# Attention of layer 1: two short runs of scores per step, each followed by value products and a sum, in place of one long run

## The chip, the cores and the metric

The kernel runs on one core of a Trainium2 chip. The metric is the device time of one execution in microseconds, here the median of three runs of the kernel before. The span that the profile shows is the time of one execution taken with the profiler on, and it stands a few microseconds beside the median.

## What is computed

Two transformer layers over 4 sequences of 1024 tokens of width 512, with 16 heads of width 32. Layer 0 has attention with a distance bias and an MLP; layer 1 quantises its weights and activations around plain attention. The change touches the attention of layer 1 alone:

```python
attn = jax.nn.softmax(jnp.einsum('bhqd,bhkd->bhqk', q, k) * hd ** (-0.5), axis=-1)
o = jnp.einsum('bhqk,bhkd->bhqd', attn, v).transpose(0, 2, 1, 3).reshape(B, T, D)
```

There are 4 x 16 = 64 heads (batch and head together), each with a 1024 x 1024 score matrix.

## The kernel before

`build_program` runs six stages one after the other, with a barrier of all engines between them. The fifth is `stage_attention1`. Each engine has a program of its own that is written out by hand in step order; engines meet at semaphores only, and each engine works through its own list in order. So the order in `tensor_program` is the order on TensorE.

A head is 8 tiles of 128 queries, and there are 512 tiles in all. A *step* w (the loop variable of every program) takes four tiles, half a head. There are 128 steps of new tiles (NW) and 7 more that empty the pipeline (TAIL).

The scores are computed twice, once for the minimum and once for the exponential:

- `score(u)`, line 720, called **S** below: the 128 x 1024 scores of a query tile, two matmuls of 512 columns, into one of two PSUM buffers `s` of two banks each. `minimum(u)` on VectorE (line 810) reduces them to one number per query and frees the buffer.
- After a head's 8 minima, `minima_halves` on GpSimd (lines 864 and 866) splits them into a high and a low part, `turn_minima` on TensorE (line 756) transposes them, `take_minima` on VectorE (line 816) copies them out, and a DMA puts them as two extra rows beside the queries.
- `score_turned(u, g)`, line 730, called **T**: keys by queries this time, one matmul of 512 columns with the minima already subtracted by the extra rows, into one of three one-bank PSUM buffers `st`. `exponential(u, g)` on ScalarE (line 796) writes exp into `PT` and frees the bank.
- `times_v(u)`, line 741, called **V**: one key block of the value product, four matmuls of the source with 32 output columns each, side by side in the array, 8 matmul instructions in the trace (each of the four is two).
- `add_pair(m)` on GpSimd (line 873) adds two key blocks of `PT`, and `total(m)`, line 749, called a **sum** below, multiplies the result with ones to get the softmax denominators, again 8 matmul instructions. V and sums of one head add up in the two halves of one bank, `po`.
- At the end of a head `take_output` (VectorE, line 823) copies `po`, `turn_output` (TensorE, line 762) transposes it in four matmuls, and `output` (VectorE, lines 833 and 837) divides.

The three `st` banks are a ring that `score_turned`, `turn_minima` and `turn_output` take in the order of their calls. Whoever takes a bank waits until its last user has been read: T waits for the exponential of the taker three places earlier.

Step w before holds, on TensorE: one long run of scores (T S T S TTT S TT S T: 8 T of tiles of step w-4 among 4 S of step w), then `turn_minima` in even steps or `turn_output` in odd ones, then four V of step w-5, and in every even step four sums. An even step is called a minima step below, an odd one an output step; in the steady part every step is one or the other.

Of the kernel before, what the change touches and what calls it, by code (L numbers as in the profile page):

```python
# [12 lines left out]
DC, FC, LT = D // P, F // P, L // P  # L13
# [381 lines left out]
QW = L // 4  # L395
HALF = LT // 2
N_HEADS = B * H
# [245 lines left out]
def stage_attention1(K):  # L643
# [6 lines left out]
    NW, TAIL = N_TILES // 4, 7  # L650
    with Stage(K, "T1") as S:
# [3 lines left out]
        pT = [S.sb(f"PT1{i}", [P, LT, L]) for i in range(2)]  # L655
# [58 lines left out]
        def score(u):  # L714
            n, t = divmod(u, LT)
            p, j = divmod(n, PAIR)
            qs, ks = qs_l.ready(pe, p), ks_l.ready(pe, p)
            ps = ps_r.take(pe, u, (s_min, u + 1))
            for g in range(L // BLK):
                op = nc.tensor.matmul(ps[:, g * BLK:(g + 1) * BLK], qs[0:ROWS, j, t * P:(t + 1) * P],  # L720
                                      ks[0:ROWS, j, g * BLK:(g + 1) * BLK], start=True, stop=True)
            op.then_inc(*s_score.up())

        def score_turned(u, g):
            n, kb = divmod(u, LT)
            p, j = divmod(n, PAIR)
            pe.wait_ge(s_row[n % 2], 32 * (n // 2 + 1))
            pe.wait_ge(s_neg, 1)
            ps = pst_r.take(pe, ("st", u, g), (s_exp, 2 * u + g + 1))
            nc.tensor.matmul(ps[:], ks_l.at[p][0][0:ROWS + 2, j, kb * P:(kb + 1) * P], qs_l.at[p][0][0:ROWS + 2, j, g * BLK:(g + 1) * BLK],  # L730
                             start=True, stop=True).then_inc(*s_st.up())

        def times_v(u):
            n, kb = divmod(u, LT)
            p, j = divmod(n, PAIR)
            v = v_l.ready(pe, p)
            pe.wait_ge(s_exp, 2 * u + 2)
            if kb == 0:
                pe.wait_ge(s_ov, n)
            for g in range(4):  # L740
                op = nc.tensor.matmul(po[g * HD:(g + 1) * HD, 0:QW], v[:, kb, j * HD:(j + 1) * HD],  # L741
                                      pT[n % 2][:, kb, g * QW:(g + 1) * QW], start=kb == 0, stop=kb == LT - 1)
            op.then_inc(*s_pv.up())

        def total(m):
            n, k = divmod(m, LT // 2)
            pe.wait_ge(s_two, m + 1)
            for g in range(4):
                op = nc.tensor.matmul(po[g * HD:(g + 1) * HD, QW:2 * QW], K.ones[:, 0:HD], two[m % 6][:, g * QW:(g + 1) * QW],
                                      start=k == 0, stop=k == LT // 2 - 1)  # L750
            op.then_inc(*s_sum.up())

        def turn_minima(n):
            ps = pst_r.take(pe, ("min", n), (s_mr, n + 1))
            pe.wait_ge(s_mm, n + 1)
            nc.tensor.transpose(ps[0:2 * LT, 0:P], mm[n % 2][:].bitcast(F32).rearrange("p a t -> p (a t)"), K.ident[:]).then_inc(*s_mt.up())

        def turn_output(n):
            ps = pst_r.take(pe, ("out", n), (s_out, n + 1))
            pe.wait_ge(s_ov, n + 1)  # L760
            for i in range(2 * QW // P):
                op = nc.tensor.transpose(ps[:, i * P:(i + 1) * P], ov[n % 2][:, i * P:(i + 1) * P], K.ident[:])
            op.then_inc(*s_turn.up())

        def tensor_program():
            n_turned = n_first = 0
            for w in range(NW + TAIL):
                for turned, first in ((1, 1), (1, 1), (3, 1), (2, 1), (1, 0)):
                    if 0 <= w - 4 < NW:
                        for _ in range(turned):  # L770
                            score_turned(*divmod(8 * (w - 4) + n_turned, 2))
                            n_turned = (n_turned + 1) % 8
                    if w < NW and first:
                        score(4 * w + n_first)
                        n_first = (n_first + 1) % 4
                n, odd = divmod(w - 2, 2)
                if not odd and 0 <= n < N_HEADS:
                    turn_minima(n)
                n, odd = divmod(w - 7, 2)
                if not odd and 0 <= n < N_HEADS:  # L780
                    turn_output(n)
                if 0 <= w - 5 < NW:
                    for i in range(4):
                        times_v(4 * (w - 5) + i)
                n, odd = divmod(w - 6, 2)
                if not odd and 0 <= n < N_HEADS:
                    for i in range(LT // 2):
                        total(n * LT // 2 + i)

        def exponential(u, g):  # L790
            n, kb = divmod(u, LT)
# [13 lines left out]
        def minimum(u):  # L805
            n, t = divmod(u, LT)
            if t == 0 and n >= 2:
                dve.wait_ge(s_mm, n - 1)
            dve.wait_ge(s_score, u + 1)
            nc.vector.tensor_reduce(mn[n % 2][:, t:t + 1], ps_r.at[u][:], AX.X, ALU.min).then_inc(*s_min.up())  # L810

        def take_minima(n):
            if n >= 2:
                dve.wait_ge(s_row[n % 2], 32 * (n // 2))
            dve.wait_ge(s_mt, n + 1)
            nc.vector.tensor_copy(mr[n % 2][:], pst_r.at["min", n][0:2 * LT, 0:P]).then_inc(*s_mr.up())

        def take_output(n):
            dve.wait_ge(s_pv, (n + 1) * LT)
            dve.wait_ge(s_sum, (n + 1) * LT // 2)  # L820
            if n >= 2:
                dve.wait_ge(s_turn, n - 1)
            nc.vector.tensor_copy(ov[n % 2][:], po[:]).then_inc(*s_ov.up())

        def output(n):
            h = n % H
            buf = og.room(dve, n // GRP)
            ps = pst_r.at["out", n]
            dve.wait_ge(s_turn, n + 1)
            if n >= 2:  # L830
                dve.wait_ge(s_out, n - 1)
            sums = ps[:, 2 * P:4 * P].rearrange("p (i g d) -> p i g d", i=2, d=HD)[:, :, :, 0]
            nc.vector.reciprocal(rec[n % 2][:], sums).then_inc(*s_rec.up())
            dve.wait_ge(s_rec, n + 1)
            hc = slice(h % GRP * HD, (h % GRP + 1) * HD)
            for i in range(2):
                op = nc.vector.tensor_tensor(buf[:].rearrange("p (g i) d -> p i g d", i=2)[:, i, :, hc],
                                             ps[:, i * P:(i + 1) * P].rearrange("p (g d) -> p g d", d=HD),
                                             rec[n % 2][:, i, :].unsqueeze(2).to_broadcast([P, 4, HD]), ALU.mult)
            op.then_inc(*s_out.up())  # L840

        def vector_program():
            for w in range(NW + TAIL):
                if w < NW:
                    minimum(4 * w)
                    minimum(4 * w + 1)
                n, odd = divmod(w - 7, 2)
                if not odd and 0 <= n < N_HEADS:
                    take_output(n)
                if w < NW:  # L850
                    minimum(4 * w + 2)
                    minimum(4 * w + 3)
                n, odd = divmod(w - 2, 2)
                if not odd and 0 <= n < N_HEADS:
                    take_minima(n)
                n, odd = divmod(w - 7, 2)
                if not odd and 0 <= n < N_HEADS:
                    output(n)

        def minima_halves(n):  # L860
            pool.wait_ge(s_min, (n + 1) * LT)
# [25 lines left out]

        sync_program()
        tensor_program()
        vector_program()  # L890
        scalar_program()
        gpsimd_program()
# [1297 lines left out]
```

## Time and profile before

| | us |
|---|---|
| median of 3 runs | 3895.55 (3895.14 to 3897.41) |
| profiled execution, span | 3899.1 |
| stage of the change, in the span | 2553 to 3523, 970 |
| TensorE busy, whole span | 3604.4 (92%) |
| VectorE / ScalarE / GpSimd busy, whole span | 2538.2 / 2259.6 / 1668.4 |

The profile gives, per engine, busy time and what an idle engine was waiting for. PE is TensorE's matmul, PEld its weight load (which may run beside a matmul), DVE VectorE, ACT ScalarE, POOL GpSimd. PE's matmuls overlap, so that a busy PE isn't a PE at its full rate. What a wait costs is better read from the starts of successive matmuls and from PEld's idle time.

### The profile page before, as it was taken

What the parts mean: (1) busy time and instruction counts of PE and PEld (TensorE: products, weight loads), DVE (VectorE), ACT (ScalarE), POOL (GpSimd) and SP (SyncE); (2) the same over time, 40 slices, a digit from 0 to 9 for tenths busy, and PEclk for the clock granted to TensorE, in tenths of its full rate; (3) what the DMA queues carried; (4) which work ended last, traced back from release to release, by engine and by line L of the source; (5) the groups of instructions that cost most, each with busy time, mean ns of one, the idle gap of its engine ahead of it and who ended that gap; (6) DMA issues with size and microseconds to landing.
All of it is one profiled execution on the core that took longest, in us unless ns stands there. A gap on an engine that the chain in (4) does not pass through costs nothing. (4 is left out here: it accounts for less than half of the span.)

```text
span 3899.1 us, 67913 instructions
## 1 busy us (share of the span) xinstructions
PE 3604.4 (92%) x25868; PEld 2519.1 (65%) x25924; DVE 2538.2 (65%) x4159; ACT 2259.6 (58%) x3899; POOL 1668.4 (43%) x1931
## 2 busy tenths in 40 slices
PE   8997999999999988699999995979999999995999
PEld 6885767677777766578778873546666666652555
DVE  4335888888888867334431116857777777765987
ACT  2225888888888856222222225835555555554988
POOL 0004555555555547000000006746666666663554
PEclk9998999999999999899999997979999999997999
DMA  5546333333333159444431116853333333414221
GB/s 188 185 162 157 64 69 64 69 64 69 64 69 63 31 174 320 134 149 159 157 130 54 54 42 212 314 122 78 74 69 74 78 69 71 81 31 136 77 82 50
DMA packets 309604, 419.91 MB, mean 108 GB/s; under 512 B 90472, under 2 KB 167788, under 8 KB 309274
## 3 DMA queue, kind: packets, MB, share of 16 engines
q1 hardware_dynamic: 309280, 415.56, 38.3%
q8 instruction: 207, 3.39, 0.4%
q14 instruction: 117, 0.96, 0.1%
HBM read 257.34 MB, written 157.32 MB: 106 GB/s over the span
## 5 line engine op out<-in xcount | busy, mean ns | idle before, releaser
L796 ACT ACTIVATE PT<-st 128x512 f32<-128x512 f32 x1024 | 545.2, 605 | 420.9 <-PE st L730 417.5
L634 POOL TENSOR_SCALAR biastile<-dist,ascale 128x1024 f32<-128x1024 f32 x512 | 577.1, 1127 | 487.3 <-DVE mn L588 474.5
L810 DVE TENSOR_REDUCE mn<-s 128x1 f32<-128x1024 f32 x512 | 596.6, 1216 | 274.1 <-PE s L720 274.0
L873 POOL TENSOR_TENSOR two<-PT 128x1024 f32<-128x1024 f32 x256 | 603.4, 2376 | 306.8 <-ACT PT L796 306.6
L588 DVE CUSTOM_DVE_ANT_0 Sn<-sp,biastile 128x1024 f32<-128x1024 f32 x512 | 622.1, 1215 | 78.4 <-PE pt L521 46.6
L559 ACT ACTIVATE Sn<-Sn,mn 128x1024 f32<-128x1024 f32 x512 | 586.8, 1146 | 19.0 <-DVE mn L588 19.0
L521 PEld LDWEIGHTS pt<-ident,Sn 128*128 128x128 f32 x4096 | 455.2, 141 | 177.5 <-issue 151.0
L521 PE MATMUL pt<-ident,Sn 128*128 128x128 f32 x4096 | 546.9, 277 | 22.0 <-DVE og L601 22.0
L549 ACT ACTIVATE PT<-pt 128x512 f32<-128x512 f32 x576 | 338.0, 599 | 135.6 <-PE pt L521 125.8
L1335 ACT ACTIVATE gf<-pf,b1T 128x512 f32<-128x512 f32 x128 | 88.3, 690 | 542.2 <-PE pf L1280 529.6
L730 PE MATMUL st<-QS,KS 98*128 98x512 f32 x1024 | 377.4, 426 | 1.2 <-ACT PT L796 1.2
L720 PE MATMUL s<-KS,QS 96*128 96x512 f32 x1024 | 353.5, 428 | 25.6 <-DMA KS<-s_khi 23.8
L551 DVE COPY PT<-pt 128x512 f32<-128x512 f32 x448 | 309.8, 692 | 88.2 <-PE pt L521 81.5
L1426 DVE TENSOR_TENSOR gl<-gf,gh 128x512 fp32r<-128x512 f32 x128 | 88.6, 692 | 381.3 <-ACT gh L1339 378.9
L1741 POOL MEMSET rcD<- 128x128 bf16 x2 | 0.3, 206 | 781.2 <-POOLq L131 781.2
L489 PE MATMUL sp<-KS,QS 97*128 97x512 f32 x1024 | 304.8, 418 | 23.6 <-DMA KS<-cpad 18.8
L510 PE MATMUL po<-PT,Vp 128*32 128x256 f32 x4096 | 273.7, 384 | 27.6 <-ACT ov L572 27.6
L730 PEld LDWEIGHTS st<-QS,KS 98*128 98x128 f32 x1024 | 192.6, 188 | 146.2 <-ACT PT L796 65.1
L741 PE MATMUL po<-PT,Vp 128*32 128x256 f32 x4096 | 248.8, 384 | 0.0
L720 PEld LDWEIGHTS s<-KS,QS 96*128 96x128 f32 x1024 | 177.2, 194 | 99.4 <-DVE mn L810 51.7
L1291 PE MATMUL pacc<-w2h,gh 128*128 128x512 f32 x512 | 203.5, 397 | 4.2 <-DVE gl L1426 4.2
L489 PEld LDWEIGHTS sp<-KS,QS 97*128 97x128 f32 x1024 | 174.2, 191 | 50.2 <-issue 19.2
(257 smaller groups left out, 6169.1 us busy)
## 6 DMA issues: line engine op xcount, KB each, us to landing
QS<-s_qhi SPq DMA_DIRECT2D x128, 256.0 KB, 4.9
KS<-s_khi SPq DMA_DIRECT2D x128, 256.0 KB, 6.8
KS<-s_klo SPq DMA_DIRECT2D x64, 256.0 KB, 6.1
QS<-s_qlo SPq DMA_DIRECT2D x64, 256.0 KB, 6.8
Vp<-s_v SPq DMA_DIRECT2D x64, 256.0 KB, 7.5
s_o<-og SPq DMA_DIRECT2D x32, 512.0 KB, 4.0
xA<-in_x SPq DMA_DIRECT2D x8, 1024.0 KB, 5.8
s_qhi<-qstage SPq DMA_DIRECT2D x32, 256.0 KB, 2.0
```

Of the source, the lines that this page charges most:

```text
L489: op = nc.tensor.matmul(ps[:, g * BLK:(g + 1) * BLK], qs[0:rows_s, j, t * P:(t + 1) * P], ks[0:rows_s, j, g * BLK:(g + 1) * BLK], start=Tr ...
L521: op = nc.tensor.transpose(ps[:, i, :], sn[:, (g * HALF + i) * P:(g * HALF + i + 1) * P], K.ident[:])
L549: nc.scalar.activation(dst, src, ACT.Copy).then_inc(*s_cp_act.up())
L551: nc.vector.tensor_copy(dst, src).then_inc(*s_cp_dve.up())
L559: nc.scalar.activation(sn[:], sn[:], ACT.Exp, scale=-1.0, bias=mn[n % 3][:, t:t + 1], accum_out=sums[n % 5][:, t:t + 1]).then_inc(*s_exp.up())
L588: nc.vector.tensor_tensor_reduce(sn[:], sp_r.at[s][:], bt[s % 2][:], 1.0, 3.4e38, ALU.add, ALU.min, m).then_inc(*s_min.up())
L634: nc.gpsimd.tensor_scalar(bt[s % 2][:], dist[:, t, :], K.ascale[:, n % H:n % H + 1], 1.0, ALU.mult, ALU.mult).then_inc(*s_bias.up())
L720: op = nc.tensor.matmul(ps[:, g * BLK:(g + 1) * BLK], qs[0:ROWS, j, t * P:(t + 1) * P], ks[0:ROWS, j, g * BLK:(g + 1) * BLK], start=True, ...
L730: nc.tensor.matmul(ps[:], ks_l.at[p][0][0:ROWS + 2, j, kb * P:(kb + 1) * P], qs_l.at[p][0][0:ROWS + 2, j, g * BLK:(g + 1) * BLK], start=Tr ...
L796: nc.scalar.activation(pT[n % 2][:, kb, g * BLK:(g + 1) * BLK], pst_r.at["st", u, g][:], ACT.Exp, scale=-1.0).then_inc(*s_exp.up())
L810: nc.vector.tensor_reduce(mn[n % 2][:, t:t + 1], ps_r.at[u][:], AX.X, ALU.min).then_inc(*s_min.up())
L873: nc.gpsimd.tensor_tensor(two[m % 6][:], pT[n % 2][:, 2 * k, :], pT[n % 2][:, 2 * k + 1, :], ALU.add).then_inc(*s_two.up())
```

## The change

The long run becomes two runs. Each has two S and four T in the order S T S T T T, then (in the first run alone) the transposes of minima or of output, then two V and one sum. Sums move from four in every second step to one in each run, one step after the step in which their head's V were all done before; they now share the bank `po` with V that are still adding, so the first sum of a head no longer starts an accumulation of its own. VectorE's order follows: `take_output` goes ahead of the step's first minimum, `output` and `take_minima` between the second and the third.

```diff
         def tensor_program():
-            n_turned = n_first = 0
             for w in range(NW + TAIL):
-                for turned, first in ((1, 1), (1, 1), (3, 1), (2, 1), (1, 0)):
-                    if 0 <= w - 4 < NW:
-                        for _ in range(turned):
-                            score_turned(*divmod(8 * (w - 4) + n_turned, 2))
-                            n_turned = (n_turned + 1) % 8
-                    if w < NW and first:
-                        score(4 * w + n_first)
-                        n_first = (n_first + 1) % 4
-                n, odd = divmod(w - 2, 2)
-                if not odd and 0 <= n < N_HEADS:
-                    turn_minima(n)
-                n, odd = divmod(w - 7, 2)
-                if not odd and 0 <= n < N_HEADS:
-                    turn_output(n)
-                if 0 <= w - 5 < NW:
-                    for i in range(4):
-                        times_v(4 * (w - 5) + i)
-                n, odd = divmod(w - 6, 2)
-                if not odd and 0 <= n < N_HEADS:
-                    for i in range(LT // 2):
-                        total(n * LT // 2 + i)
+                for run in range(2):
+                    for k in range(4):
+                        if k < 2 and w < NW:
+                            score(4 * w + 2 * run + k)
+                        if 0 <= w - 4 < NW:
+                            score_turned(*divmod(8 * (w - 4) + 4 * run + k, 2))
+                    if run == 0:
+                        n, odd = divmod(w - 2, 2)
+                        if not odd and 0 <= n < N_HEADS:
+                            turn_minima(n)
+                        n, odd = divmod(w - 7, 2)
+                        if not odd and 0 <= n < N_HEADS:
+                            turn_output(n)
+                    if 0 <= w - 5 < NW:
+                        times_v(4 * (w - 5) + 2 * run)
+                        times_v(4 * (w - 5) + 2 * run + 1)
+                        total(2 * (w - 5) + run)
...
         def vector_program():
             for w in range(NW + TAIL):
+                n, odd = divmod(w - 7, 2)
+                out = not odd and 0 <= n < N_HEADS
+                if out:
+                    take_output(n)
                 if w < NW:
                     minimum(4 * w)
                     minimum(4 * w + 1)
-                n, odd = divmod(w - 7, 2)
-                if not odd and 0 <= n < N_HEADS:
-                    take_output(n)
+                if out:
+                    output(n)
+                m, odd = divmod(w - 2, 2)
+                if not odd and 0 <= m < N_HEADS:
+                    take_minima(m)
                 if w < NW:
                     minimum(4 * w + 2)
                     minimum(4 * w + 3)
```

In `total` the matmuls' `start=k == 0` becomes `start=False`; in it and in `times_v` a flag for the build's own bookkeeping is set, which is no instruction.

## Rows read from the trace of the kernel before

**Rows 1.** Busy time by stretch: the stage, and ten pairs of steps (all engines)

```profile
core 0: us, PE busy (x) PEld busy (x) DVE busy (x) ACT busy (x) POOL busy (x), PEclk, DMA share, GB/s
2553.00:3523.00 970.00, 960.00 (x8512) 582.93 (x8512) 680.40 (x830) 545.19 (x1024) 628.14 (x385) 0.98 0.34 70
...
3100.00:3247.00 147.00, 147.00 (x1338) 90.27 (x1330) 106.21 (x130) 85.30 (x160) 97.90 (x60) 1.00 0.35 72
```

**Rows 2.** Waits in two pairs of steps, 2999.53 to 3028.93: total us, times, longest

```profile
PEld st L730 <- ACT PT L796: 1.9, 8, 0.3
PEld st L730 <- issue: 1.6, 4, 0.4
PEld s L720 <- DVE mn L810: 1.3, 6, 0.3
```

**Rows 3.** Timeline of PE, an output step: start, us until its last end, xcount

```profile
3011.95 0.50 PE L730 MATMUL st<-QS,KS 98*128 98x512 f32 x1
3012.29 0.63 PE L720 MATMUL s<-KS,QS 96*128 96x512 f32 x2
3012.76 0.39 PE L730 MATMUL st<-QS,KS 98*128 98x512 f32 x1
...
3013.45 0.89 PE L730 MATMUL st<-QS,KS 98*128 98x512 f32 x3
...
3016.18 0.60 PE L762 MATMUL st<-ident,ov 128*128 128x128 f32 x4
3016.71 0.42 PE L741 MATMUL po<-PT,Vp 128*32 128x256 f32 x4
```

**Rows 4.** Timeline of PE, the end of the minima step before it

```profile
3008.16 0.27 PE L756 MATMUL st<-ident,mm 128*16 128x128 f32 x1
3008.36 1.93 PE L741 MATMUL po<-PT,Vp 128*32 128x256 f32 x32
3010.11 1.91 PE L749 MATMUL po<-two,ones 128*32 128x256 f32 x32
```

**Rows 5.** Timeline of weight loads in the output step, with idle time before each

```profile
3011.95 0.19 PEld L730 LDWEIGHTS st<-QS,KS 98*128 98x128 f32 x1 [0.41 <-issue]
...
3015.08 0.19 PEld L730 LDWEIGHTS st<-QS,KS 98*128 98x128 f32 x1 [0.30 <-ACT PT L796]
...
3016.06 0.48 PEld L762 LDWEIGHTS st<-ident,ov 128*128 128x128 f32 x4 [0.16 <-ACT PT L796]
```

**Rows 6.** Timeline of ScalarE in the output step

```profile
3012.57 1.22 ACT L796 ACTIVATE PT<-st 128x512 f32<-128x512 f32 x2 [3.62 <-PE st L730]
3013.95 3.04 ACT L796 ACTIVATE PT<-st 128x512 f32<-128x512 f32 x6 [0.15 <-PE st L730]
```

**Rows 7.** Timeline of VectorE in the output step

```profile
3012.96 2.36 DVE L810 TENSOR_REDUCE mn<-s 128x1 f32<-128x1024 f32 x2 [3.21 <-PE s L720]
3015.23 0.68 DVE L823 COPY ov<-po 128x512 f32<-128x512 f32 x1
```

**Rows 8.** Timeline of GpSimd, 3000 to 3018

```profile
3000.41 4.70 POOL L873 TENSOR_TENSOR two<-PT 128x1024 f32<-128x1024 f32 x2 [3.37 <-ACT PT L796]
...
3005.36 0.20 POOL L866 TENSOR_TENSOR mm<-mn,mm 128x8 fp32r<-128x8 f32 x1
...
3015.11 4.72 POOL L873 TENSOR_TENSOR two<-PT 128x1024 f32<-128x1024 f32 x2 [3.37 <-ACT PT L796]
```

**Rows 9.** Timeline of PE, step 5, where V follows T directly

```profile
2589.63 0.39 PE L730 MATMUL st<-QS,KS 98*128 98x512 f32 x1
2589.95 1.93 PE L741 MATMUL po<-PT,Vp 128*32 128x256 f32 x32
```

**Rows 10.** Timeline of PE, step 128: eight T without S between them

```profile
3489.12 0.96 PE L730 MATMUL st<-QS,KS 98*128 98x512 f32 x3
3490.39 2.51 PE L730 MATMUL st<-QS,KS 98*128 98x512 f32 x5 [0.31 <-ACT PT L796]
```

**Rows 11.** The V of step 128 as a stretch: us, PE busy, PEclk, DMA share, GB/s

```profile
3493.15:3496.33 3.18, 3.18 (x33) 0.54 0.14 38
```

More of the change, by code:

```diff
@@ L741, in times_v @@
                 op = nc.tensor.matmul(po[g * HD:(g + 1) * HD, 0:QW], v[:, kb, j * HD:(j + 1) * HD],
-                                      pT[n % 2][:, kb, g * QW:(g + 1) * QW], start=kb == 0, stop=kb == LT - 1)
+                                      pT[n % 2][:, kb, g * QW:(g + 1) * QW], start=kb == 0, stop=kb == LT - 1,
+                                      skip_group_check=True)
             op.then_inc(*s_pv.up())
@@ L749, in total @@
                 op = nc.tensor.matmul(po[g * HD:(g + 1) * HD, QW:2 * QW], K.ones[:, 0:HD], two[m % 6][:, g * QW:(g + 1) * QW],
-                                      start=k == 0, stop=k == LT // 2 - 1)
+                                      start=False, stop=k == LT // 2 - 1, skip_group_check=True)
             op.then_inc(*s_sum.up())
@@ L852, in vector_program @@
                     minimum(4 * w + 3)
[L853 to L858, printed above, removed]
         def minima_halves(n):
```

## The prediction, made before the changed kernel ran

> **What bounds the kernel now.** I read the stretches of busy time first. The stage of the change takes 970 us of the span, and TensorE is busy for 960 of them; VectorE, the next, for 680 [rows 1]. Ten pairs of steps take 147.0 us, so a pair (a minima step and an output step) takes 14.70 us, at a granted clock of 1.00; per pair VectorE works 10.6 us, GpSimd 9.8 and ScalarE 8.5 [rows 1]. No other engine can set the pace by its load. But a busy matmul row says nothing of the rate, so the waits come second. In two pairs the score runs' weight loads waited 1.9 us for exponentials, 1.3 us for minima, and 1.6 us for "issue", that is, for nothing that the profile names [rows 2]. The last stands 4 times, once per step, and one of them is the way back from V and sums to the scores [rows 5]: the engine changes from 32 output columns to 128 there, and from 128 to 32 on the way in. Such a change is called a border below.
>
> So the change buys a shorter queue of scores (fewer waits for ScalarE and VectorE) and pays with more borders. Third, the timelines give the price of each. All times below count from the start of the first score matmul of a run.
>
> **What the rows give.** *Spacing in a run:* T, S, S start at 3012.76 and the next T at 3013.45, 0.23 each [rows 3]. *V and sums:* 32 instructions of V take 1.75 us from start to start of what follows, 32 of the sums 1.84 up to the next score [rows 3, 4]. A fourth of it is 0.44 for one V and 0.43 for one sum; the sums' 1.84 has about 0.11 of border in it. *The border in:* T directly before V takes 0.32 [rows 9] where T before a score takes 0.23, so 0.09. *The border out:* these 0.11, and then 0.34 from the first score matmul to the second (3011.95 to 3012.29 [rows 3]) in place of 0.23, 0.11 more. With 0.02 for V's slower first group a round trip costs 0.33 us.
>
> The first weight load after the border starts at 3011.95, together with its matmul and after 0.41 us idle [rows 5]; nothing was loaded ahead. The Trainium skill, page "TensorE: Matmul & The Clock Gate", section "Step-by-step: what each phase is for", has TensorE pull a weight load ahead of matmuls in flight when it goes to the background weight buffer. By that rule the border would be all but free and the added time 40 us less than in my sum (60 pairs x 2 borders x 0.33). The trace disagrees here, and another page, "TensorEngine Tiling (Array Packing)", section "Key Properties", says that changing the tiling mode drains the engine, which is what the row shows.
>
> *ScalarE's answer:* a T's exponential starts 0.43 us after the T (3012.76 to the second of the pair at 3013.19), 0.49 where a wait for another semaphore stands ahead (3013.45 to 3013.95), takes 0.60, and exponentials in a row start 0.49 apart [rows 3, 6]. The bank's next weight load starts 0.05 later: the fourth exponential ends at 3015.04, the load is at 3015.08 [rows 5, 6]. For the transpose the matmul comes 0.12 after its load [rows 3, 5]. *VectorE's answer:* a minimum starts 0.43 after the second matmul of its S and takes 1.2 [rows 3, 7]. *GpSimd:* a pair addition starts 0.07 after the fourth exponential's end and takes 2.36 to 2.39; the split of the minima ends 0.45 after the addition ahead of it (3005.11 to 3005.56) [rows 6, 8].
>
> **A check on these prices:** the minima step before, by the same steps. T0 0; S 0.34, 0.57; T1 0.81; S 1.04, 1.27; T2 to T4 1.50, 1.74, 1.98. The third S waits for the first minimum, 0.57 + 0.43 + 1.22 + 0.05 = 2.29, against 2.21 without. T5 2.86, T6 3.13; the fourth S waits for the second minimum, 3.47; T7 3.99; transpose 4.22; V 4.43; sums 6.18; end 8.02. The output step is 4.22 + 0.53 (four transposes to V, 3016.18 to 3016.71 [rows 3]) + 1.86 = 6.61. Together 14.63 against 14.70 measured.
>
> **The change, part by part, for a pair.**
> Removed and added instructions: none of weight. Every S, T, V, sum and transpose is there before and after, and VectorE, ScalarE and GpSimd do the same work. `rows_to_queries` and the loads on SP wait for the same events, of which the minima come earlier; each head's T are two steps away, so nothing hangs on it. A head's first sum without its own start flag is no other instruction.
> *Without any wait* a run is S T S T T T: S 0, 0.34; T0 0.57; S 0.81, 1.04; T1 1.27; T2 1.51; T3 1.74. A second run then has V at 2.06, and two V, a sum and the border take 0.88 + 0.43 + 0.11 = 1.43 (with the first group): 3.49. The first run of an output step: transposes at 1.97, V at 2.50, end 3.93. Of a minima step: transpose 1.97, V 0.20 later [rows 4] at 2.17, end 3.60. The pair: 3.60 + 3.93 + 2 x 3.49 = 14.51. So even with no wait left, the gain is 0.19 per pair: the two new round trips (0.66) eat most of the 0.85 that waits cost now (14.70 less 14.51 - 0.66).
> *Added wait 1, T3 in each run.* It takes T0's bank. T0 0.57 + 0.49 + 0.60 + 0.05 = 1.71 for its load, the matmul about 0.08 later: 1.79 in place of 1.74. I take 0.05 x 4 runs = 0.20 (bounds 0 and 0.3).
> *Added wait 2, the transposes.* Before, two T and two S stood between them and the T whose bank they take. Now T2 and T3 alone do. T1 1.27 + 0.43 = 1.70, + 0.60 = 2.30, + 0.05 load, + 0.12 matmul = 2.47, against 1.79 + 0.23 = 2.02: **0.45 per step, 0.9 per pair**. Eight T with nothing between them show this wait already: the fourth comes 1.27 after the first and waited 0.31 [rows 10]. What is queued behind it on TensorE is all of the rest, V and the next run. Bounds: 0.35 (if the small load of the minima is faster) and 0.5 each.
> *Added wait 3, the minima's split.* The transpose of the minima moves from the end of the step to its first half, and GpSimd's list has the split behind the pair additions of the step before. In the second run of a step the exponentials start 1.06, 1.70, 2.18, 2.67, so the last ends at 3.27; GpSimd adds from 3.34 to 5.73, which is 2.19 into the next step (a second run is 3.49 + 0.05 = 3.54); the split ends at 2.64, and the transpose starts at about 2.80 in place of 2.47. That is 0.33 per pair. Bounds 0 (if the addition starts earlier) and 0.5.
> *VectorE:* `take_output` copies `po` from 0.2 to 0.9 of an output step (0.68 [rows 7]), ahead of the transposes; the first minimum moves by 0.1, and the third S comes over 4 us after the first. `output` ends near 4.2, and the T that wants its bank comes at 5.9. Cost nothing; if the cover went, some 0.1 us.
> Sum per pair: 14.51 + 0.20 + 0.90 + 0.33 = 15.94, or 1.24 more than 14.70. Steps 8 to 127 are 60 pairs: +74 to +75 us, and I take 75. Filling and emptying: steps 5 to 7 lose about 2 us (added borders), the last five win about 2 (T in fours, not eights, wait less for ScalarE [rows 10]), both estimates. Nothing net.
> 3899.1 + 75 = 3974 for the profiled execution; the median lies 3.5 lower, so 3895.6 + 75 = **3971**.
>
> **Rivals.**
> *B, the split of the minima isn't late* (GpSimd starts its additions earlier than I think), or T3 doesn't wait: 15.4 to 15.65 per pair, +42 to +57 us, 3938 to 3953. For it: GpSimd has 6 us per pair free. Against: it can't start before the fourth exponential.
> *C, not slower: the waits vanish.* Short runs are what three banks can hold, and with 14.51 per pair the kernel would be 11 us faster, 3884. It decides at the transposes: they must find T1's bank free within 0.75 us of T1, where the rows give 1.08. Waits of under 0.19 per pair in all are the point of break-even. Little speaks for it.
> *D, the border is hidden by the load ahead:* 40 us less than the forecast, 3931.
> *E, the clock falls.* In all of the 147 us above it is 1.00 (2.4 GHz) [rows 1]. Where eight T in a row were paced by ScalarE at the end [rows 10], it fell to the 1.2 GHz level, and the V after that took 3.18 us at 0.54 [rows 11] in place of 1.75 [rows 4]. If one step in eight ran so, each would lose about 4 us, +64 on top, 4035. The same page of the Trainium skill, section "A second HAM failure mode: psum-queue depth-cycling", tells of such a clock going up and down from small idle times between groups of matmuls. By it this change, which adds idle time, would get E. Against: the pair now has 0.85 us of waits and 0.66 us of borders with no fall; with the change it has 1.43 and 1.32 us in 15.9.
> *F, further waits that I don't see* (VectorE's new order, semaphores on TensorE): another 0.3 or more per pair, 3990 to 4010.
>
> **Chances:** forecast (3957 to 3988) 0.64, B 0.16, C 0.04, D 0.03, E 0.03, F 0.07, no difference 0.03. The range of 3936 to 3992 takes in B and the bounds of the waits, and leaves out some 0.17. A measurement of this kernel tells about 0.2% (8 us) from no change: faster 0.04, within it 0.03, slower 0.93.
>
> **What the changed profile would show.** A pair of steps of 15.9 to 16.0 us. The idle time of "issue" at the borders 4 times per step in place of 2. Weight loads of the transposes (lines for minima and output) waiting 0.4 to 0.8 us each, the longest for ScalarE and GpSimd; hardly any wait of S for minima. A second run of 3.5 us. I would be wrong if the transposes didn't wait (then 3880 to 3910), if T3 waited much longer than 0.05, or if the granted clock in the steady part were below 1.00.

## The result and the profile after

| | before | changed |
|---|---|---|
| median | 3896.48 (4 runs) | 3971.67 (3969.42 to 3974.57, 4 runs) |
| ratio | | 1.0194, interval 1.0179 to 1.0208 |
| profiled execution, span | 3899.1 | 3967.6 |
| stage, first score to last output transpose | 2559.0 to 3522.5, 963.5 | 2551.8 to 3590.7, 1038.9 |
| a pair of steps, steady part | 14.71 | 15.93 |

The changed kernel is 75.2 us slower, and the stage is 75.4 us longer. The profiled spans differ by 68.5 alone: in the changed kernel's profile the stage begins 7.2 us earlier, after code that the change doesn't touch. In the ten kept profiles, all with the same code ahead of the stage, it begins anywhere from 2547.5 to 2559.0. A span's difference holds such scatter of other stages; the pair of steps, 60 times repeated, doesn't, and is what the experiments below are read from.

The stretches of the changed kernel answer to [rows 1]; columns are length, busy time of PE, PEld, DVE, ACT and POOL, granted clock, DMA share, GB/s. TensorE is now without work for 0.6 us of a pair. Each of the other engines is busy for much the same time per ten pairs as before (VectorE 108.2 us against 106.2, ScalarE 87.0 against 85.3, GpSimd 99.0 against 97.9):

```profile
3100.00:3259.30 159.30, 153.22 (x1331) 89.25 (x1331) 108.17 (x130) 86.97 (x160) 98.96 (x61) 1.00 0.33 69
2999.92:3015.84 15.92, 15.32 (x137) 8.93 (x133) 10.80 (x13) 8.69 (x16) 9.92 (x7) 1.00 0.03 5
```

The waits of two pairs, 2999.92 to 3031.77, answer to [rows 2]:

```profile
PEld st L730 <- ACT PT L792: 2.2, 8, 0.3
PEld s L720 <- issue: 2.1, 5, 0.4
PEld st L757 <- ACT PT L792: 1.5, 2, 0.8
...
PEld po L741 <- issue: 1.3, 6, 0.2
PEld s L720 <- DVE mn L806: 1.2, 3, 0.4
PE st L757 <- POOL mm L862: 1.0, 2, 0.5
PEld st L763 <- ACT PT L792: 0.9, 2, 0.4
```

The two transposes (L757 minima, L763 output) now wait, the minima's for GpSimd in the end. The row "DVE mn" is not what it says. Call the border from V and sums back to scores or transposes the way out, and the one into V the way in: two rows of the weight loads' timeline show the same 0.41 us at the way out, once put to "issue" and once to a minimum that had ended at 3007.41, half a microsecond before. The 5 and the 3 together are the 8 ways out of four steps, where before there were 4. So no score waits for a minimum any more.

```profile
3004.28 0.30 PEld L720 LDWEIGHTS s<-KS,QS 96*128 96x128 f32 x2 [0.41 <-issue]
...
3007.87 0.30 PEld L720 LDWEIGHTS s<-KS,QS 96*128 96x128 f32 x2 [0.41 <-DVE mn L806]
```

The timeline of PE over the pair (start, us until its last end, xcount) answers to [rows 3] and [rows 4]. The four runs start at 2999.92, 3004.28, 3007.87 and 3012.24, and the next pair at 3015.84:

```profile
2999.92 0.73 PE L720 MATMUL s<-KS,QS 96*128 96x512 f32 x2
3000.49 0.39 PE L730 MATMUL st<-QS,KS 98*128 98x512 f32 x1
3000.73 0.62 PE L720 MATMUL s<-KS,QS 96*128 96x512 f32 x2
3001.19 0.97 PE L730 MATMUL st<-QS,KS 98*128 98x512 f32 x3
3002.65 0.27 PE L757 MATMUL st<-ident,mm 128*16 128x128 f32 x1 [0.49 <-POOL mm L862]
3002.85 1.07 PE L741 MATMUL po<-PT,Vp 128*32 128x256 f32 x16
...
3004.28 0.73 PE L720 MATMUL s<-KS,QS 96*128 96x512 f32 x2
...
3005.56 0.95 PE L730 MATMUL st<-QS,KS 98*128 98x512 f32 x3
3006.44 1.07 PE L741 MATMUL po<-PT,Vp 128*32 128x256 f32 x16
...
3007.87 0.73 PE L720 MATMUL s<-KS,QS 96*128 96x512 f32 x2
...
3010.22 0.66 PE L763 MATMUL st<-ident,ov 128*128 128x128 f32 x4
3010.81 1.07 PE L741 MATMUL po<-PT,Vp 128*32 128x256 f32 x16
...
3012.24 0.73 PE L720 MATMUL s<-KS,QS 96*128 96x512 f32 x2
```

GpSimd's timeline shows why the minima's transpose is late [rows 8]. The addition of the step before ends at 3002.05, 2.13 us into the step; the split ends at 3002.50, and the transpose runs at 3002.65:

```profile
2999.67 2.38 POOL L869 TENSOR_TENSOR two<-PT 128x1024 f32<-128x1024 f32 x1 [1.98 <-ACT PT L792]
3002.02 0.20 POOL L860 TENSOR_SCALAR mm<-mn 128x8 fp32r<-128x8 f32 x1
3002.30 0.20 POOL L862 TENSOR_TENSOR mm<-mn,mm 128x8 fp32r<-128x8 f32 x1
```

### The profile page after: what moved, and what is told of

Same layout as the page of the kernel before. It is cut to its first block and busy times, and to the rows that moved or that the text cites. A ratio compares the mean times of both kernels' runs of the same rounds, so it can differ in the third digit from the quotient of the medians.

```text
span 3967.6 us, 67969 instructions
## 1 busy us (share of the span) xinstructions
PE 3640.0 (92%) x25924; PEld 2507.2 (63%) x25924; DVE 2552.0 (64%) x4159; ACT 2270.3 (57%) x3899; POOL 1674.9 (42%) x1931
## 5 line engine op out<-in xcount | busy, mean ns | idle before, releaser
L792 ACT ACTIVATE PT<-st 128x512 f32<-128x512 f32 x1024 | 556.0, 598 | 487.3 <-PE st L730 483.1
L730 PE MATMUL st<-QS,KS 98*128 98x512 f32 x1024 | 350.6, 423 | 2.4 <-ACT PT L792 2.4
L510 PE MATMUL po<-PT,Vp 128*32 128x256 f32 x4096 | 273.7, 384 | 27.6 <-ACT ov L572 27.6
L741 PE MATMUL po<-PT,Vp 128*32 128x256 f32 x4096 | 274.9, 386 | 0.0
```

The costliest lines, as they stand in the source:

```text
L792: nc.scalar.activation(pT[n % 2][:, kb, g * BLK:(g + 1) * BLK], pst_r.at["st", u, g][:], ACT.Exp, scale=-1.0).then_inc(*s_exp.up())
```

## Experiments

The theory M is the prediction's sum: two new borders per pair, and three new waits that more than take the place of those removed. Its main rival is that the borders alone carry the loss (and its opposite, D, that they cost nothing). "Pair" is the mean over 50 pairs in the steady part; medians of the first four stand against a kernel before of 3893.38 us on their chip, those of the last four against 3894.97.

| kernel | pair, expected | pair, measured | median | over before |
|---|---|---|---|---|
| x4_border | 15.25 to 15.35 | 15.22 | 3924.79 | 1.0078 (1.0063 to 1.0093) |
| x1_turns_later | 14.9 | 14.79 | 3897.22 | 1.0009 (1.0000 to 1.0018) |
| x5_minima_later | 15.57 | 15.57 | 3944.95 | 1.0131 (1.0116 to 1.0146) |
| x2_t_first | 15.2 | 15.21 | 3925.18 | 1.0080 (1.0063 to 1.0097) |
| x8_both | 14.40 | 14.41 | 3877.86 | 0.9953 (0.9941 to 0.9966) |
| x3_tfirst_min_later | 14.51 | 14.55 | 3883.47 | 0.9970 (0.9961 to 0.9980) |
| x7_sums_in_fours | 16.36 | 16.37 | 3997.96 | 1.0264 (1.0250 to 1.0278) |
| after_again | 15.93 | 15.92 | 3966.82 | 1.0188 (1.0172 to 1.0203) |

### The border by itself

On the kernel before:

```diff
-                n, odd = divmod(w - 2, 2)
-                if not odd and 0 <= n < N_HEADS:
-                    turn_minima(n)
-                n, odd = divmod(w - 7, 2)
-                if not odd and 0 <= n < N_HEADS:
-                    turn_output(n)
-                if 0 <= w - 5 < NW:
-                    for i in range(4):
-                        times_v(4 * (w - 5) + i)
+                for run in range(2):
+                    if run:
+                        n, odd = divmod(w - 2, 2)
+                        if not odd and 0 <= n < N_HEADS:
+                            turn_minima(n)
+                        n, odd = divmod(w - 7, 2)
+                        if not odd and 0 <= n < N_HEADS:
+                            turn_output(n)
+                    if 0 <= w - 5 < NW:
+                        for i in range(2):
+                            times_v(4 * (w - 5) + 2 * run + i)
```

> The kernel before, its one long run of scores and its sums kept; only the transposes of minima and output move from the end of the scores to between the second and the third V, so that every step has one more change from 32 output columns to 128 and back, and nothing else new. My sum (a round trip costs 0.27 to 0.33 us per step, 128 steps): a pair of steps of 15.25 to 15.35 us, +35 to +42 us on before, 3932 to 3938. If weight loads hide the border (rival D): within 8 us of before. If the borders carried the whole +75 of the change (two more in it than in before per pair, as here), this kernel would be 75 us slower, 3971.

Measured: a pair of 15.22, +0.51, so 0.26 per round trip, and +31 us. It is a little under the low end of my price, and it is not zero: D falls, and so does the rival that the borders carry all 75 us. PE's timeline shows both ways. V starts 0.33 after the T; 16 V instructions take 1.00 us from start to start of the transposes, where in the changed kernel 16 V take 0.88 or 0.89 before sums, which need no border. Against the kernel before, that is 0.10 on the way in and about 0.12 on the way out. The four output transposes up to V then take 0.59 in place of 0.53, the minima's one 0.20 (3012.07 to 3012.27) as before. A border out to a transpose is therefore a little cheaper than one out to a score, where the first matmul takes 0.11 longer to the second:

```profile
3003.76 0.40 PE L730 MATMUL st<-QS,KS 98*128 98x512 f32 x1
3004.09 1.07 PE L741 MATMUL po<-PT,Vp 128*32 128x256 f32 x16
3005.09 0.66 PE L762 MATMUL st<-ident,ov 128*128 128x128 f32 x4
3005.68 1.07 PE L741 MATMUL po<-PT,Vp 128*32 128x256 f32 x16
3006.68 0.50 PE L730 MATMUL st<-QS,KS 98*128 98x512 f32 x1
```

### Transposes at the start of the second run

On the changed kernel, `turn_minima` and `turn_output` go ahead of the loop over k, for the second run:

```diff
                 for run in range(2):
+                    if run == 1:
+                        n, odd = divmod(w - 2, 2)
+                        if not odd and 0 <= n < N_HEADS:
+                            turn_minima(n)
+                        n, odd = divmod(w - 7, 2)
+                        if not odd and 0 <= n < N_HEADS:
+                            turn_output(n)
                     for k in range(4):
...
-                    if run == 0:
-                        n, odd = divmod(w - 2, 2)
-                        if not odd and 0 <= n < N_HEADS:
-                            turn_minima(n)
-                        n, odd = divmod(w - 7, 2)
-                        if not odd and 0 <= n < N_HEADS:
-                            turn_output(n)
```

> The changed kernel, with the transposes of minima and of output taken from the end of the first run of scores to the start of the second run. The number of borders stays; the transposes now find their bank free and the minima's split done (added waits 2 and 3 gone). My sum: a pair is 4 x 3.59 + 0.44 + 0.11 = 14.9 us in place of 15.92, 61 us less than the changed kernel, about 3911, still 13 to 16 over before. If the borders carry the loss and the waits are nothing: no change from the changed kernel, 3972.

Measured: a pair of 14.79, 1.14 less than the changed kernel, and a median 3.8 us over before. With every border left in place, nearly the whole loss is gone. So the waits before the transposes are what makes the change slow, and the borders are paid by what the short runs save. It came out 0.11 lower than my sum: the minima's transpose at this place costs 0.03 us up to the next score in place of the 0.11 that I gave it, and the four output transposes 0.41 (3012.26 to 3012.67) in place of 0.44. So of the 1.14 some 0.1 comes from a cheaper place for the transposes (they stand there behind a border that is paid anyway) and the rest from the waits:

```profile
3005.05 0.28 PE L757 MATMUL st<-ident,mm 128*16 128x128 f32 x1
3005.09 0.70 PE L720 MATMUL s<-KS,QS 96*128 96x512 f32 x2
```

### The minima's transpose alone, at the end of the second run

```diff
-                    if run == 0:
-                        n, odd = divmod(w - 2, 2)
-                        if not odd and 0 <= n < N_HEADS:
-                            turn_minima(n)
-                        n, odd = divmod(w - 7, 2)
-                        if not odd and 0 <= n < N_HEADS:
-                            turn_output(n)
+                    n, odd = divmod(w - 2, 2)
+                    if run == 1 and not odd and 0 <= n < N_HEADS:
+                        turn_minima(n)
+                    n, odd = divmod(w - 7, 2)
+                    if run == 0 and not odd and 0 <= n < N_HEADS:
+                        turn_output(n)
```

On the changed kernel, and in `vector_program` `take_minima` goes behind the step's last minimum.

> The changed kernel, with the transpose of the minima alone moved from the first run of scores to the end of the second (and VectorE's copy of them behind the step's last minimum). The wait for the bank stays, the wait for GpSimd's split goes. My sum: the first run of a minima step 3.59, its second 1.74 + 0.61 + 0.20 + 1.43 = 4.0, together 7.6 in place of 7.95: 0.35 per pair, 21 us less than the changed kernel, about 3951. If GpSimd's lateness is only another face of the wait for the bank: no change, 3972.

Measured: 15.57, 0.36 less. GpSimd's lateness is a wait of its own, of the size that I gave it. The transpose at its new place still waits for its bank: it comes 1.08 us after T1, the first of the three T in the row, where three spacings would be 0.70:

```profile
3010.88 0.97 PE L730 MATMUL st<-QS,KS 98*128 98x512 f32 x3
3011.96 0.28 PE L757 MATMUL st<-ident,mm 128*16 128x128 f32 x1
```

### T first in each run

On the changed kernel:

```diff
                     for k in range(4):
-                        if k < 2 and w < NW:
-                            score(4 * w + 2 * run + k)
                         if 0 <= w - 4 < NW:
                             score_turned(*divmod(8 * (w - 4) + 4 * run + k, 2))
+                        if k < 2 and w < NW:
+                            score(4 * w + 2 * run + k)
```

> The changed kernel with each run in the order T S T S T T in place of S T S T T T. The first exponentials start 0.4 us earlier against the end of the run, so T3 and the output transposes no longer wait for their banks (added waits 1 and 2 gone), while the minima still wait for GpSimd's split, by less. My sum: second runs 3.49, first run of an output step 3.93, of a minima step 4.29: a pair of 15.2 us, 43 us less than the changed kernel, about 3929, 32 over before. If the two borders explain the loss: no change from the changed kernel, 3972. If VectorE matters in the short runs: it gets its scores 0.23 later, and the kernel would be slower than the changed one.

Measured: 15.21, 0.72 less, by nothing but which matmul stands first. T0, whose bank T3 takes, now comes 0.57 earlier against the end of the run, and T1, whose bank the transposes take, 0.46 earlier. The output's first transpose follows T3 at the usual spacing; the minima's still waits 0.51, which the view puts to ScalarE. The exponential of T1 had ended at 3014.20, and GpSimd's split, the last row, ends at 3014.86, 0.14 before the transpose. So it was the split:

```profile
3006.43 0.63 PE L730 MATMUL st<-QS,KS 98*128 98x512 f32 x2
3006.90 0.60 PE L763 MATMUL st<-ident,ov 128*128 128x128 f32 x4
...
3015.00 0.27 PE L757 MATMUL st<-ident,mm 128*16 128x128 f32 x1 [0.51 <-ACT PT L792]
```

```profile
3012.98 1.22 ACT L792 ACTIVATE PT<-st 128x512 f32<-128x512 f32 x2 [1.04 <-PE st L730]
...
3014.66 0.20 POOL L862 TENSOR_TENSOR mm<-mn,mm 128x8 fp32r<-128x8 f32 x1
```

### All waits away: two kernels under the kernel before

The first is x2_t_first with the transposes moved as in x1_turns_later, the second x2_t_first with the minima's transpose moved as in x5_minima_later.

> The changed kernel with the transposes at the start of the second run and each run in the order T S T S T T: both changes of the runs before, so that no wait for a bank or for GpSimd should be left and the new borders alone remain. My sum: 4 x 3.49 + 0.41 + 0.03 = 14.40 us per pair, against 14.71 before and 15.93 changed: 19 us under the kernel before, ratio 0.995. If ScalarE's or VectorE's latency finds a new place to bind: 14.7 or more per pair, ratio 1.000 or above.

> The changed kernel with the order T S T S T T, output transposes still at the end of the first run, minima transposes at the end of the second. This is the changed kernel's structure at the no-wait sum of my prediction, 14.51 us per pair (3.93 + 3.49 + 3.49 + 3.60): 12 us under the kernel before, ratio 0.997. If the transposes still wait for a bank by 0.1 us or more each: 14.7 per pair, ratio 1.000.

Measured: 14.41 and 14.55 per pair, 17 and 12 us under the kernel before. x8_both is four runs of 3.49 us plus 0.41 for the output transposes and 0.03 for the minima's. The rows show the three ways in which its runs start: with the output transposes (0.41 to the first T), straight behind a sum (T 0.54 after the sum's start), and with the minima's transpose. That transpose stands 0.55 after the sum's start, where a T would have stood, and the T follows 0.03 later:

```profile
2999.76 0.66 PE L763 MATMUL st<-ident,ov 128*128 128x128 f32 x4
3000.17 0.48 PE L730 MATMUL st<-QS,KS 98*128 98x512 f32 x1
...
3003.11 0.61 PE L750 MATMUL po<-two,ones 128*32 128x256 f32 x8
3003.65 0.50 PE L730 MATMUL st<-QS,KS 98*128 98x512 f32 x1
...
3006.60 0.61 PE L750 MATMUL po<-two,ones 128*32 128x256 f32 x8
3007.15 0.28 PE L757 MATMUL st<-ident,mm 128*16 128x128 f32 x1
3007.18 0.48 PE L730 MATMUL st<-QS,KS 98*128 98x512 f32 x1
```

The idea of the change, shorter runs for a short ring, does pay, once nothing at the end of a run wants a bank back too soon. The gain is small (0.3% and 0.5%), but both intervals lie under 1. These two kernels have the spread sums too; the short runs without them, in this order, weren't run.

### Sums in fours, as before the change

In `tensor_program` the change runs two of a head's four sums one step earlier than before, and the other two in the step in which all four stood; no sum comes a step later, as the section on the change can be read. Put back, on the changed kernel:

```diff
-                        total(2 * (w - 5) + run)
+                    n, odd = divmod(w - 6, 2)
+                    if run == 1 and not odd and 0 <= n < N_HEADS:
+                        for i in range(LT // 2):
+                            total(n * LT // 2 + i)
```

> The changed kernel with the sums grouped as before, four at the end of each minima step and none in the other runs; runs, borders and V stay. The same work, but the output step's second run is 0.43 us shorter (3.16), so GpSimd's split of the minima comes 0.43 later into the minima step, and the transpose that waits for it too. My sum: 15.93 + 0.43 = 16.36 per pair, 26 us more than the changed kernel, 1.9 + 0.7 = 2.6% over before. If where the sums stand makes no difference: the changed kernel's time, 1.9% over before. If moving the sums was itself a cost of the change: less than that.

> The changed kernel itself, on the same chip as the three others. 15.93 us per pair of steps and a ratio of 1.019 to the kernel before, as measured first; the other runs are set against this one.

Measured: 16.37 against 15.92, 0.45 more per pair, and the medians are 31 us apart where 60 pairs make 27. TensorE has the same instructions and the same borders, only 0.43 us less of them between the output step's last T and the minima step's transpose, and this 0.43 appears whole in the wait: 0.94 in place of 0.49.

```profile
3011.10 0.27 PE L757 MATMUL st<-ident,mm 128*16 128x128 f32 x1 [0.94 <-POOL mm L865]
```

GpSimd in the same stretch: the split ends at 3010.95, 0.15 before the transpose.

```profile
3008.12 2.39 POOL L872 TENSOR_TENSOR two<-PT 128x1024 f32<-128x1024 f32 x1 [1.56 <-ACT PT L795]
3010.48 0.19 POOL L863 TENSOR_SCALAR mm<-mn 128x8 fp32r<-128x8 f32 x1
3010.75 0.20 POOL L865 TENSOR_TENSOR mm<-mn,mm 128x8 fp32r<-128x8 f32 x1
```

So spreading the sums was no cost of the change; it made the loss smaller, by making TensorE later and so its wait for GpSimd shorter.

## Why the prediction came out right

The forecast was 3971, the measured median 3971.67. The pair was to be 15.94 and is 15.92 in its timeline. By its steps, in us:

| | predicted | measured |
|---|---|---|
| first run of a minima step | 4.43 | 4.36 |
| first run of an output step | 4.43 | 4.37 |
| second runs | 3.54 | 3.59, 3.60 |
| start of the minima's transpose | 2.80 | 2.73 |
| start of the output's transposes | 2.47 | 2.35 |
| addition of the step before ends, into the next | 2.19 | 2.13 |

*The sum without waits* (14.51) was right: x3_tfirst_min_later has the same number of borders and transposes between scores and V, with the waits gone, and shows 14.55. Its order differs (T first, the minima's transpose in the second run), which the prices without waits don't tell apart.

*Added wait 1, T3's bank,* was mis-sized: 0.05 expected, 0.10 paid. T3 starts at 1.74 as if nothing had held it, but its weight load waited 0.26 and starts with it, and it takes about 0.50 in place of 0.39. The loss shows one instruction later, V coming 0.42 after T3 (3006.02 to 3006.44) where T to V alone is 0.32 [rows 9]. It makes second runs 0.05 longer than I said.

```profile
3006.01 0.19 PEld L730 LDWEIGHTS st<-QS,KS 98*128 98x128 f32 x1 [0.26 <-ACT PT L792]
3006.44 0.59 PEld L741 LDWEIGHTS po<-PT,Vp 128*32 128x32 f32 x16 [0.24 <-issue]
```

*Added wait 2, the transposes' bank,* was right in place and a little too high. The output's transposes start at 2.35 with their load, where I had put the load at 2.35 and the matmul 0.12 behind it, and the first of them then takes 0.17 to the second in place of 0.11; so 0.06 less than I counted in all. x2_t_first, which takes waits 1 and 2 away together, gave 0.72.

*Added wait 3, GpSimd's split,* was right: 0.36 in x5_minima_later against 0.33. The terms don't add freely, though. With wait 2 gone as well it is worth 0.66 (15.21 to 14.55), since the two stand at the same instruction and the later one hides the other.

*The borders* were priced at 0.33 per round trip from the kernel before; x4_border shows 0.26 there, where the way out leads to a transpose. For the way out to a score my price fits: the runs of 3.49 us in x8_both are made with it. What makes the border cost that time no run shows. The row that the prediction read as the engine being drained shows that no weights were loaded ahead, and not why.

*The rivals.* B (no lateness of GpSimd) fell by the changed kernel's own timeline and by x5_minima_later; C's idea that waits vanish fell for this kernel and holds for the two kernels that were built for it; D fell by x4_border. E's clock didn't fall in the steady part: it is 1.00 over ten pairs. The Trainium skill, page "TensorE: Matmul & The Clock Gate", section "A second HAM failure mode: psum-queue depth-cycling", warns of it for small idle times between groups; the trace doesn't agree for the idle times of this kernel's steady part, up to 0.8 us in front of a transpose. The 4 us that E charged for each fall had no row behind it. Just behind the steady part the clock did fall in this profile: V and the sum behind the minima's transpose of step 128 took 2.72 us (3560.51 to 3563.23) at 0.50, the 1.2 GHz level. In after_again, the same kernel, they took 1.43 us at 1.00.

F's VectorE order had no visible cost: `take_output` ends at 3008.77, 0.90 into the step, the transposes that need it run 1.45 later. That order wasn't tried by itself.

```profile
3008.08 0.69 DVE L819 COPY ov<-po 128x512 f32<-128x512 f32 x1 [0.68 <-PE po L750]
```

*Slips that changed little:* in the check of the prices 0.57 + 0.43 + 1.22 + 0.05 is 2.27 and not 2.29; the third S came at 2.36 there (3003.87 to 3006.23). The 0.49 from T0 to its exponential is 0.52 in the changed kernel (3000.49 to 3001.01), so that T3's load comes at 1.74 and not at 1.71. Idle times of "issue" at the borders were foretold 4 times per step; four steps show 14, the 8 ways out and 6 of the ways in.

*Where luck had a part:* second runs were 0.05 or 0.06 longer than said and first runs 0.06 or 0.07 shorter. These errors cancel to 0.02 per pair, about 1 us in all. And 60 pairs at 15.93 in place of 14.71 make 73.3 us of the stage's 75.4, where I took 75 for them. The other 2.1 come from filling and emptying, which I had put at nothing net: up to the start of step 128 the stage lost 2.4 us beyond the pairs, as estimated, but from there on it won only 0.35 in place of 2, with the fall of the clock in it. In after_again, without that fall, it won 1.9 (33.03 to 31.12 us from the start of step 128 to the last output transposes). The kernel before has a fall there too, which cost it 1.4 (3.18 us [rows 11] in place of 1.75), so only some 0.5 of the 1.9 is left for the shorter groups of T. Last, measured again, the changed kernel was 71.9 us over the kernel before and not 75.2, so a hit to within 1 us is more than such a sum can promise.

## What to carry to other kernels

A ring of n banks asks one question of every order: how long is it from a taker's place back to the one n places before? Splitting a long run in two shortens this distance at each run's end, and what was hidden there (here a transpose) then waits for an exponential that has only begun. Before splitting, move such takers behind the other work, where their bank is long free, and let the first instruction of each run be the one whose consumer has the longest chain; the same division in two runs then went from 1.9% slower to 0.5% faster here. A move forward in one engine's list also has to be checked against the list of the engine that feeds it: GpSimd's split stood right behind an addition that ended 2.1 us into the step.

## What the runs showed of the hardware that I had not expected

- A transpose with 16 columns of weights at the head of a run, right after the way out of 32-column matmuls, costs 0.03 us (x8_both): it starts at 3007.15 and the next matmul at 3007.18. Four transposes of 128 columns at the same place cost 0.41.
- A matmul whose weights weren't loaded ahead is recorded as starting together with its load, and what this costs shows in the start of the next matmul: 0.17 in place of 0.11 after a transpose, 0.34 in place of 0.23 after a score, 0.42 in place of 0.32 from T3 to V.
- A round trip between 128 and 32 output columns costs 0.26 us where the way out leads to a transpose (x4_border).
- The granted clock can fall in one execution of a kernel and not in another: behind the minima's transpose of step 128 it was 0.50 in the changed kernel's first profile and 1.00 in its second.
